# One block for three stages: last sums inverted later, an activation ahead of a root, another order text

## The chip, the cores and the metric

The kernel runs on one core of a Trainium2 chip. The metric is the device time of one execution, in microseconds (us), from start to end on that core. Five engines work side by side, each on its own queue of instructions: TensorE (PE), VectorE (DVE), ScalarE (ACT), GpSimd (POOL) and SyncE (SP, which only issues transfers). They meet only through semaphores. A block holds one list of instructions for each engine, and at its end all engines drain and wait for each other before the next block begins.

## The reference

Four sequences of 2048 rows of 256 numbers go through attention and then through two of eight experts. Cut to what matters:

```python
def _layernorm(x, axis=-1, eps=1e-05):
    m = jnp.mean(x, axis=axis, keepdims=True)
    v = jnp.var(x, axis=axis, keepdims=True)
    return (x - m) / jnp.sqrt(v + eps)

# attention: 16 heads of 16, causal
q = (x @ wq + bq).reshape(b, s, H, HD).transpose(0, 2, 1, 3)   # k, v alike
scores = jnp.where(causal, jnp.einsum('bhqd,bhkd->bhqk', q, k) * SCALE, -jnp.inf)
out = jnp.einsum('bhqk,bhkd->bhqd', jax.nn.softmax(scores, axis=-1), v)
return out.transpose(0, 2, 1, 3).reshape(b, s, d) @ wo + bo

# experts: the two best of 8 by the first row of each sequence
_, idx = jax.lax.top_k(x[:, 0, :] @ Wr + br, 2)
h = jax.nn.gelu(jnp.einsum('bsd,bkde->bkse', x, W1[idx]) + b1[idx][:, :, None, :], approximate=False)
o = jnp.einsum('bkse,bkef->bksf', h, W2[idx]) + b2[idx][:, :, None, :]
return jnp.sum(o, axis=1) / 2

x = x + _layernorm(attention(_layernorm(x)))
x = x + _layernorm(experts(_layernorm(x)))
```

## The kernel before, in words

The rows are cut into 16 chunks of 512 (four per sequence), numbered n = 0 to 15, with b = n // 4 and c = n % 4.

**Stage A** (`stage_a`) normalises each chunk, multiplies it by wq, wk and wv, and stores the products in DRAM. **Stage B** (`stage_b`) is the attention: eight pairs of groups of four heads each. PE multiplies queries and keys twice. The first product (line 622, into the tile b_ring of three banks) is only for the row maxima, which DVE takes with `tensor_reduce` (line 632, into b_pmax). The second (line 1392, into b_psS) gives the scores, ACT takes their exponentials (line 1349), and PE multiplies them with the values (line 1409, into b_psO). There are 640 steps of values.

In which order PE works these off is written out by hand in the text `ORDERS`, and every engine of stage B walks through the same text: 0 and 1 are a quarter of a score step in the upper or lower half of the array, a and b a maximum unit in that half, v a step of values, and p, q, r, y and l are pieces of the front. The **front** (class `Front`) is the beginning of stage C for the first sequence, run in the tail of stage B: p projects half a chunk, q and r take square roots, y turns half of a normalised chunk, l scores the experts.

The sums of the exponentials come out as a column of the values. For each pair, SP loads them (`load_sums`, line 231), DVE inverts them (`invert_sums`, line 236), SP stores the inverses (`store_inverses`, line 240). For the last pair this is done at the start of stage C.

**Stage C** (`stage_c`) has one step for each chunk n. PE: `hidden(n)` (line 1763, 16 multiplications into the two banks of c_psH, four pieces i), `outer(n)` (line 1776), `turn_y(n + 2)` (line 1742), `project(n + 4)` (line 1733). ACT: `gelu(n)` (line 1684, one activation per piece), the roots (line 99) of the chunks ahead, `copy_y(n + 2)` (line 1709), `root_ffn(n)` (line 99). DVE: `normalise_x1(n + 2)`, `add_attention(n + 3)`, `experts_end(n)` (lines 1616 to 1623 and the variance of the result), `take_projection(n + 4)`, `experts_out(n)`. PE's third piece of `hidden(n)` waits for the first gelu of the same chunk, because there are two banks. Gelu and square root lie in different tables of ACT, and between them a table is loaded (ACT_TABLE_LOAD).

Stages A and B share one block, and stage C has its own. ACT's last work in stage B is the copy of the last b_psO (line 1359) and a gelu of one column (line 1378) that brings the gelu table. ACT's first instruction in stage C is `act.sem_inc(gelu_done, 2)` (line 1711), for which the first piece of `hidden(0)` waits:

```python
            nc.scalar.activation(ready[:, :], consts.eps[:, :], ACT.Gelu)   # end of stage B
            ...
            act.sem_inc(gelu_done, 2)                                       # start of stage C
            for b, c in STEPS:
                n = b * NC + c
                if n < UNLED:
                    gelu(b, c, n)
                if ahead(b, c, 3):
                    roots(*ahead(b, c, 3))
                if ahead(b, c, 2):
                    copy_y(*ahead(b, c, 2))
                if n >= UNLED - 1 and n < LAST:
                    gelu(*ahead(b, c, 1))
                root_ffn(b, c, n)
```

With UNLED = 14, ACT's order at the end is gelu(12), roots(15), copy_y(14), root_ffn(12), gelu(13), copy_y(15), gelu(14), root_ffn(13), gelu(15), root_ffn(14), root_ffn(15).

Of the kernel before, what the change touches and what calls it, by code (L numbers as in the profile page):

```python
# [259 lines left out]
class Groups:  # L260
# [7 lines left out]
    def __init__(self, nc, ctx, qk_scr, v_scr):  # L268
        self.nc, self.qk_scr, self.v_scr = nc, qk_scr, v_scr
        self.ones_set = ctx.enter_context(nc.semaphore("g_ones_set"))  # L270
        self.ones_laid = ctx.enter_context(nc.semaphore("g_ones_laid"))
# [7 lines left out]
        self.nmax_set = ctx.enter_context(nc.semaphore("b_nmax_set"))  # L279
        self.vS = ctx.enter_context(nc.sbuf_tensor("g_v", [P, 2, NT, VROW], F32))  # L280
        self.loaded = [ctx.enter_context(nc.semaphore(f"g_loaded{p}")) for p in range(2)]
        self.early = [ctx.enter_context(nc.semaphore(f"g_early{h}")) for h in range(2)]
# [68 lines left out]
NPAIR = B * NG // 2  # L351
# [72 lines left out]
def leads_of(n):  # L424
# [9 lines left out]
    "0b011ab01a010a110aa010a1vba1010b0011v0101b0011b0101a1010bv01ab01vb0101a1010bbvb0101a101ab0v0b0b0101bav1a"  # L434
    "1a1010abva110b01b100bvab010101a10v1010a1100a10100b01a1va1010bva1010b010b1ava1010ba1010bv1a100b010b1ab010"
    "1abva1010b0101abvb0101ab0101ava1010ba1010bvba10101010bbbvab1010ab0110ba1010bv1a1b00101a0va11100010ba10b0"
    "1avvb01av1a1a100bb0v0101abb0101v01010101v0b1a10b0101ava1010b0101abv1a0b01010ba1vb0101a10b01avb0101a101a0"
    "bva1010b01a10bva1010b011ab0va10101a10b0bvb0101a1010bavba101a10100avab01010101av01010ba110a0101a1010bv10b"
    "a10v0b01a10101bva1b0010011av1ab0010101b1010vb0101ava10b011a100bva1010ba1010bva1010b0b011ab0101bavb00101a"
    "bva110b001a1vab0101001a1v10100b011a1a10b0v10b01ava1010a101a0bvb0101a1010bav1a101a100b0bvb0101aa1010bva10"  # L440
    "10b0101abva1010b0101abv1ab0101010bav1a0b100b0ba1a1v1a1010ba1v0b01ab010v10101ab001a10101010aav0101abv011a"
    "101abv0b0b0101abv1a1a010b010bavb0101a1010bav0b1a10b0101avb0101a1010bava1010b0101bava1010b0101abva1010b01"
    "01abvb01010b01a1avb0101a1010bava1010ba1010bv1a1001ab010bvb0010101a1av10101ab001b010101a10bv010b1bb0101bv",
    "10101ab010v0101ab0101b101010b0va1a1010bvb0101bb0101bv1a10b0101a0bva1010b011ab0va1010ba1vab010b0va110101a"
    "b0vb001a11010v1010ba10101010bavva1010b0b01a1va1010b01a10bvb0101a101ab0v1a100b01a10bva1010b01b0a1va1010b0"
    "101aavba1001ba1010bav0b011aa101ab0v01010ba101av1ab0101010v0101ab0101b01010101av1a0b10bb0101av1a100b0101a"
    "bva1010b01a10bv1a10b0101ab0vb0101a1010bav0b01a10101abvb01010b01ava101a10bv0b0b1010bav1a1a10b01ava1010ba1"
    "010bvb0101a1010bavb0101a10b01av0b0110b1a1b0vb001010ba11v10101a100aa1010101a0bva110b0v0b01a10101av0101ab0"
# [12 lines left out]
    "v0b1a010b1aa0ba1v1a100b1a10b0v1ab010b00v1a1b001a1v10101010aa10101a10b0v1a100bav1a10b00101abv1a0b01010ba1"
    "va1010b0101abv0b1a1010b01avb0101a1010bava1010b0101bava1010b0101abva1010b0101abvb01010b01a1avb0101ab0101a"
    "va1010b0101abvb0101a1010bava110101abv0b0010ba1v10101a100a01010b01a1vba1010v",
    "0ba101010b1va110b0001a1v10100ba1010101bavvb01010ba101avb0101a1010bavb0101a100ba1vb0101ab0101avb001a1101b"
    "0bvb00101a110av1010ab001110100b01a1vb0101abv1a0101a10b0bva1010b0101abva10101ab010bva1010b0101abvb0101a10"
    "10bbvab0101a1a10b0v0bb1a101a0b10ab0101v1010bab0va110b001a1v10101010bava11100010ba0101ava1010ba1vba1010b0"
    "10v1a0b01a1010bva1010b0101abv0b1a10b0101avb0101a1010bava1010b010b1av0b01a1a1010bvb0101a100ba1vb01a101010"
    "bavb0101ab0101ava1010b0101abvb0101a101a0bvb001a11a1va1b0010b0v0101ba1100b01010101bvb0011abv010ba10101vb0"
    "a1101010av0101a1010ba1010bvva1010b011ab0vb0101a0b01a1va1010b01a10bvb0101a1010bavb0011ba0101b1010bvba1010"
    "101a0v0101a1010ba1010bvvb0101ab0101av0b011a1a100bva1010ba1010bvb0101a1010bavb0101a10b01av0ba1010101abv1a"  # L470
    "010b1a010bbabv1a0b01a10b10b110b0bv0ba1101010bav0101ab0101v1a1100100ba1010bva1010bb010a1v0b011aa1010bva10"
    "10ba1010bv1a0b010b01a1va1010b0101abvb0101a1a100bv0b01a10101abva1010b0b011ava10101a10b0bva1010ba1010bvb01"
# [1366 lines left out]
```

## Time and profile before

| what | us |
|---|---|
| median of 3 runs | 1967.99 |
| lowest and highest | 1967.27 and 1971.41 |
| the profiled execution's own time | 1965.89 |
| its span, first to last instruction | 1964.20 |
| PE busy in the span | 1933.7 |
| DVE busy in the span | 1781.1 |
| ACT busy in the span | 1363.1 |

Stage A takes the first 210 us, stage B goes on to 1665.7 us, and stage C to the end. The profiled execution has 1.7 us around its span. Its ends of multiplications are modelled, so that PE can be shown busy while it goes slower than it could.

### The profile page before, as it was taken

What the parts mean: (1) busy time and instruction counts of PE and PEld (TensorE: products, weight loads), DVE (VectorE), ACT (ScalarE), POOL (GpSimd) and SP (SyncE); (2) the same over time, 40 slices, a digit from 0 to 9 for tenths busy, and PEclk for the clock granted to TensorE, in tenths of its full rate; (3) what the DMA queues carried; (4) which work ended last, traced back from release to release, by engine and by line L of the source; (5) the groups of instructions that cost most, each with busy time, mean ns of one, the idle gap of its engine ahead of it and who ended that gap; (6) DMA issues with size and microseconds to landing.
All of it is one profiled execution on the core that took longest, in us unless ns stands there. A gap on an engine that the chain in (4) does not pass through costs nothing. (4 is left out here: it accounts for less than half of the span.)

```text
span 1964.2 us, 39436 instructions
## 1 busy us (share of the span) xinstructions
PE 1933.7 (98%) x15684; PEld 848.7 (43%) x15684; DVE 1781.1 (91%) x3574; ACT 1363.1 (69%) x1655; POOL 295.1 (15%) x358
## 2 busy tenths in 40 slices
PE   9999999999999999999999999999999998999997
PEld 6655333333333333333333333333333342667665
DVE  7877899999999999999999999999999985799984
ACT  5766777777777777777777777777777768333432
POOL 4332201011111101010111111010101121322000
PEclk9999999999999999999999999999999999999999
DMA  6876716050415224050504152240505223344321
GB/s 179 252 230 201 151 39 105 7 95 9 94 27 82 52 48 90 14 94 8 94 9 94 26 82 56 45 86 17 93 7 109 80 75 120 85 127 126 94 72 43
DMA packets 151706, 162.93 MB, mean 83 GB/s; under 512 B 58466, under 2 KB 124386, under 8 KB 151522
## 3 DMA queue, kind: packets, MB, share of 16 engines
q1 hardware_dynamic: 146658, 151.98, 33.5%
q0 software_dynamic: 4864, 8.44, 1.8%
q8 instruction: 123, 2.02, 0.5%
q14 instruction: 61, 0.50, 0.1%
HBM read 100.03 MB, written 60.29 MB: 82 GB/s over the span
## 5 line engine op out<-in xcount | busy, mean ns | idle before, releaser
L632 DVE TENSOR_REDUCE b_pmax<-b_ring 128x1 f32<-128x512 f32 (+3 forms) x2264 | 1316.9, 645 | 45.6 <-PE b_ring L622 32.2
L1349 ACT ACTIVATE b_prob<-b_psS 128x1024 f32<-128x1024 f32 (+3 forms) x1280 | 1084.4, 895 | 334.4 <-PE b_psS L1392 330.6
L1392 PE MATMUL b_psS<-g_qT,g_kT 64*128 64x512 bf16 (+7 forms) x5120 | 809.3, 346 | 7.0 <-ACT b_prob L1349 5.5
L622 PE MATMUL b_ring<-g_kT,g_qT 64*128 64x512 bf16 (+3 forms) x2478 | 705.2, 347 | 0.1
L1409 PE MATMUL b_psO<-b_prob,g_v 128*32 128x512 f32 (+3 forms) x5120 | 596.4, 540 | 0.3 <-POOL b_prob L1319 0.3
L1392 PEld LDWEIGHTS b_psS<-g_qT,g_kT 64*128 64x128 bf16 (+1 forms) x5120 | 291.5, 94 | 315.9 <-ACT b_prob L1349 178.3
L622 PEld LDWEIGHTS b_ring<-g_kT,g_qT 64*128 64x128 bf16 x2478 | 221.4, 94 | 384.0 <-DVE b_pmax L632 317.4
L1319 POOL TENSOR_SCALAR_AFFINE_SELECT b_prob<-b_prob 128x512 f32<-128x512 f32 x256 | 163.0, 637 | 1281.6 <-ACT b_prob L1349 1281.4
L620 PE MATMUL b_ring<-later,query_of 64*128 64x128 bf16 x982 | 186.0, 219 | 0.8 <-ACT a_v L1104 0.5
L1409 PEld LDWEIGHTS b_psO<-b_prob,g_v 128*32 128x32 f32 x5120 | 102.9, 108 | 167.7 <-issue 131.3
L1763 PE MATMUL c_psH<-c_yT,c_w1e 128*128 128x512 f32 x256 | 116.2, 603 | 9.9 <-ACT c_hT L1684 7.3
L1173 PE MATMUL a_psQK<-c_cc,a_w 128*128 128x512 f32 x256 | 115.8, 599 | 1.2 <-ACT c_cc L1093 1.2
L1776 PE MATMUL c_psO<-c_w2e,c_hT 128*128 128x256 f32 x512 | 113.4, 380 | 0.0
L620 PEld LDWEIGHTS b_ring<-later,query_of 64*128 64x128 bf16 x982 | 85.5, 94 | 46.3 <-DVE b_pmax L632 20.8
L1776 PEld LDWEIGHTS c_psO<-c_w2e,c_hT 128*128 128x128 f32 x512 | 97.0, 190 | 18.7 <-issue 6.2
L1684 ACT ACTIVATE c_hT<-c_psH,c_b1e 128x512 f32<-128x512 f32 x64 | 43.2, 687 | 54.0 <-PE c_psH L1763 53.9
L1763 PEld LDWEIGHTS c_psH<-c_yT,c_w1e 128*128 128x128 f32 x256 | 48.3, 192 | 68.2 <-issue 52.2
L1173 PEld LDWEIGHTS a_psQK<-c_cc,a_w 128*128 128x128 f32 x256 | 47.1, 190 | 54.8 <-issue 53.8
L632 DVE TENSOR_REDUCE b_pmax<-a_ring 128x1 f32<-128x512 f32 (+4 forms) x72 | 42.3, 629 | 20.5 <-PE a_ring L622 20.5
L1187 PE MATMUL a_psV<-a_w,c_cc 128*128 128x256 f32 x256 | 60.4, 383 | 0.0
L99 ACT ACTIVATE c_ln_x_std<-c_ln_x_var,eps 128x4 f32<-128x4 f32 x12 | 3.6, 297 | 74.5 <-DVE c_ln_x_var L95 74.5
L982 DVE TENSOR_TENSOR a_parts<-c_inv,a_parts 128x2048 bf16<-128x2048 f32 x16 | 36.7, 2291 | 19.3 <-ACT a_parts L978 19.3
(162 smaller groups left out, 1058.6 us busy)
## 6 DMA issues: line engine op xcount, KB each, us to landing
qk_parts<-a_parts SPq DMA_DIRECT2D x64, 384.0 KB, 4.5
g_qT<-qk_parts SPq DMA_DIRECT2D x184, 128.0 KB, 4.7
g_kT<-qk_parts SPq DMA_DIRECT2D x184, 128.0 KB, 6.1
out_sums<-b_outT SPq DMA_DIRECT2D x64, 256.0 KB, 3.3
v_ones<-a_v SPq DMA_DIRECT2D x16, 544.0 KB, 5.7
g_v<-v_ones SPq DMA_DIRECT2D x32, 272.0 KB, 5.8
a_x<-in_L_attn_x SPq DMA_DIRECT2D x16, 512.0 KB, 5.2
c_x<-in_L_attn_x SPq DMA_DIRECT2D x15, 512.0 KB, 4.8
```

What stands on the lines that cost most here:

```text
L620: self.nc.tensor.matmul(to[:, w - P:w], consts.query_of[half:half + HALF, :], consts.later[half:half + HALF, :], start=True, stop=False, s ...
L622: ins_ = self.nc.tensor.matmul(to, groups.qT[own, g, h // 2, 0, t * P:(t + 1) * P], groups.kT[own, g, h // 2, 0, pc * CH:pc * CH + w], sta ...
L632: self.nc.vector.tensor_reduce(pmax[:, c % 2].rearrange("p (h t) n -> p h t n", t=TT)[:, heads[0]:heads[-1] + 1:2, qt, pc], bank[:, 0:k * ...
L1173: ins_ = nc.tensor.matmul(psQK[:, i % 2], w[:, t, k, m * P:(m + 1) * P], xT[:, n % 2, k], start=(k == 0), stop=(k == KD - 1))
L1187: ins_ = nc.tensor.matmul(psV[:, t], xT[:, n % 2, k, t * P:(t + 1) * P], w[:, 2, k], start=(k == 0), stop=(k == KD - 1))
L1319: nc.gpsimd.affine_select(out=tile, in_=tile, compare_op=ALU.is_ge, fill=0.0, base=0, pattern=[[0, HG], [1, P]], channel_multiplier=-1).th ...
L1349: nc.scalar.activation(prob[:, j % PBUF, 2 * s:2 * s + 2, off:CH], psS[:, 2 * s:2 * s + 2, off:CH], ACT.Exp).then_inc(exp_done, 1)
L1392: ins_ = nc.tensor.matmul(psS[:, 2 * s + p, off:CH], kT[own, g, s, ab, kt * P:(kt + 1) * P], qT[own, g, s, ab, c * CH + off:(c + 1) * CH], ...
L1409: ins_ = nc.tensor.matmul(psO[h * VW:(h + 1) * VW, off:CH], vS[:, g, kt, h * VC:h * VC + VW], prob[:, j % PBUF, h, off:CH], start=(kt == 0 ...
L1684: nc.scalar.activation(hT[:, e, m], psH[:, i % 2], ACT.Gelu, bias=experts[b % 2].b1[:, e, m:m + 1]).then_inc(gelu_done, 1)
L1763: ins_ = nc.tensor.matmul(psH[:, i % 2], experts[b % 2].w1[:, e, k, m * P:(m + 1) * P], yT[:, k, c], start=(k == 0), stop=(k == KD - 1))
L1776: ins_ = nc.tensor.matmul(psO[:, t], hT[:, e, m, t * P:(t + 1) * P], experts[b % 2].w2[:, e, m], start=(i == 0), stop=(i == 2 * KD - 1))
```

## The change

- `stage_c` gets the block of the other stages instead of one of its own, and all semaphores are now taken for the whole program. PE's first `hidden` waits for all turned pieces of the front and its choice of experts, and DVE's first `normalise_x1` for the turned pieces. The third chunk's input gets a semaphore of its own (`third_ld`), and SP's wait on the old one in `load_next_inputs` goes.
- `invert_sums` of the last pair moves from the start of DVE's stage C to the first step, between `add_attention(3)` and `experts_end(0)`.
- UNLED becomes 13: ACT's order at the end is gelu(12), roots(15), copy_y(14), **gelu(13)**, **root_ffn(12)**, copy_y(15), gelu(14), and the rest as before.
- `ORDERS` is another text with the same number of each sign.

```diff
-    def __init__(self, nc, ctx, qk_scr, v_scr):
+    def __init__(self, nc, ctx, sems, qk_scr, v_scr):
...
-    "b00v1010b0101ab0101ava0101a1010bav1a100b0101abv1a10b01010bav1a100b01a10bva1010b0101abvb01010b0b11bb01101"
-    "01a0vpp01010101vpp00110011vpp10101010v10101010vqp10101010v0101vv10101010v0101v01010101vrp01011010v101010"
-    "10vyy10100101vl01010101v10101010vyy10101010v01011010v01010101v1010101001010101v01010101v10101010vvv",
+    "b01010b111100vpp10101100vpp10100101vpp01010101v10101010vqp0101vv01010101v1010v01010101v01010101vrp010101"
+    "01v01011010vyy10101010vl01010101v01010101vyy01010101v10101010v0101010110100101v10101010v10101010vvv",
...
+        self.third_ld = sem("f_third_ld")
...
-            sp.dma_start(self.attn[:, :, :], self.chunks.x_t[2]).then_inc(self.chunks.x_ld[0], 16)
+            sp.dma_start(self.attn[:, :, :], self.chunks.x_t[2]).then_inc(self.third_ld, 16)
...
-        sp.wait_ge(self.chunks.x_ld[0], 2 * 16)
...
-        v.wait_ge(chunks.x_ld[c % 2], (c // 2 + 1) * 16)
+        if c == 2:
+            v.wait_ge(self.third_ld, 16)
+        else:
+            v.wait_ge(chunks.x_ld[c % 2], (c // 2 + 1) * 16)
...
-def stage_c(nc, consts, chunks, front, out):
+def stage_c(nc, block, sems, consts, chunks, front, out):
...
-        UNLED = LAST - 1
+        UNLED = LAST - 2
...
-        block = ctx.enter_context(nc.Block())
...
-                v.wait_ge(x_ld[c % 2], (b * 2 + c // 2 + 1) * 16)
+                v.wait_ge(x_ld[c % 2], (b * 2 + c // 2 + c % 2) * 16)
...
                 wait_for(v, y_turned, n - TURNED)
+                if n == TURNED:
+                    v.wait_ge(front.turned, 2 * TURNED)
...
-            chunks.invert_sums(v, NPAIR - 1)
             for b, c in STEPS:
...
                 n = b * NC + c
+                if n == 0:
+                    chunks.invert_sums(v, NPAIR - 1)
                 if n < LAST:
...
                     pe.wait_ge(w1_ld, (b + 1) * 16 * W_LOADS)
+                if n == 0:
+                    pe.wait_ge(front.turns_copied, 2 * TURNED)
+                    pe.wait_ge(idx_done, 1)
                 wait_for(pe, yT_done, n + 1 - TURNED)
...
+        block = outer.enter_context(nc.Block())
         with ExitStack() as ctx:
-            groups = Groups(nc, ctx, qk_scr, v_scr)
+            groups = Groups(nc, ctx, outer, qk_scr, v_scr)
             maxima = Maxima(nc, outer, consts, groups, nm_scr)
-            block = ctx.enter_context(nc.Block())
...
-        stage_c(nc, consts, chunks, front, out)
+        stage_c(nc, block, outer, consts, chunks, front, out)
```

## Rows read from the trace of the kernel before

**Rows 1.** Windows of stage B: PE, PEld, DVE, ACT, POOL busy; PEclk, DMA share, GB/s.

```profile
600.00:900.00 300.00, 299.41 (x2885) 110.09 (x2883) 289.04 (x519) 230.35 (x279) 33.11 (x52) 1.00 0.32 57
900.00:1200.00 300.00, 299.22 (x2870) 111.50 (x2866) 287.13 (x513) 232.36 (x279) 31.84 (x50) 1.00 0.28 51
1200.00:1500.00 300.00, 299.33 (x2904) 109.76 (x2903) 289.44 (x515) 231.16 (x284) 36.93 (x58) 1.00 0.32 61
```

**Rows 2.** Costliest groups, whole span: the maxima on DVE.

```profile
L632 DVE TENSOR_REDUCE b_pmax<-b_ring 128x1 f32<-128x512 f32 (+3 forms) x2264 | 1316.9, 645 | 45.6 <-PE b_ring L622 32.2
```

**Rows 3.** Timeline of PE after the join: start, us, line, idle before and releaser.

```profile
1668.25 8.73 PE L1763 MATMUL c_psH<-c_yT,c_w1e 128*128 128x512 f32 x16 [2.61 <-ACTq L1711]
...
1692.73 3.70 PE L1763 MATMUL c_psH<-c_yT,c_w1e 128*128 128x512 f32 x8 [1.07 <-ACT c_hT L1684]
...
1725.76 7.03 PE L1763 MATMUL c_psH<-c_yT,c_w1e 128*128 128x512 f32 x16
```

**Rows 4.** Timeline of ACT at the join.

```profile
1666.31 1.28 ACT L1378 ACT_TABLE_LOAD   x1
1667.61 0.20 ACT L1378 ACTIVATE b_ready<-eps 128x1 f32<-128x1 f32 x1
```

**Rows 5.** Lines 1807, 1711, 1568: queue instructions, ns min/median/max, first and last start.

```profile
L1807 ACTq DRAIN  x1: 2114/2114/2114, 1665.7 to 1665.7; - x1
L1711 ACTq EVENT_SEMAPHORE  x1: 17/17/17, 1668.1 to 1668.1; - x1
L1568 POOLq EVENT_SEMAPHORE  x4: 17/17/17, 1668.0 to 1668.4; - x4
```

**Rows 6.** Timeline of POOL at the join.

```profile
1668.19 9.26 POOL L1569 TENSOR_TENSOR c_cc<-c_cc,c_inv 128x1024 f32<-128x1024 f32 x4 [3.03 <-POOLq L1807]
```

**Rows 7.** Windows of 1 and 2 us, columns as in group 1.

```profile
1667.00:1668.00 1.00, 0.00 (x0) 0.00 (x0) 0.00 (x0) 0.80 (x2) 0.00 (x0) 1.00 0.68 262
...
1669.00:1670.00 1.00, 1.00 (x2) 0.33 (x1) 0.00 (x0) 0.00 (x0) 1.00 (x1) 0.50 0.04 11
...
1914.00:1916.00 2.00, 0.37 (x1) 0.30 (x2) 1.97 (x5) 1.99 (x3) 0.00 (x0) 1.00 0.00 0
```

**Rows 8.** Timeline of DVE in step 0 of stage C.

```profile
1670.94 0.95 DVE L236 RECIPROCAL b_pair_sums<-b_pair_sums 128x128 f32<-128x128 f32 x1 [22.62 <-DMA b_pair_sums<-out_sums]
1679.54 0.18 DVE L104 RECIPROCAL f_ln_x_rstd<-f_ln_x_std 128x4 f32<-128x4 f32 x1 [7.65 <-ACT f_ln_x_std L99]
...
1686.00 0.16 DVE L95 TENSOR_TENSOR f_ln_x_var<-f_ln_x_tmp 128x4 f32<-128x4 f32 x1
```

**Rows 9.** Timeline of PE in steps 13 and 14.

```profile
1909.19 3.60 PE L1763 MATMUL c_psH<-c_yT,c_w1e 128*128 128x512 f32 x8
1915.63 3.70 PE L1763 MATMUL c_psH<-c_yT,c_w1e 128*128 128x512 f32 x8 [2.84 <-ACT c_hT L1684]
...
1926.08 1.04 PE L1742 MATMUL c_psT<-ident,c_y 128*128 128x128 f32 x8
```

**Rows 10.** Timeline of ACT in steps 12 and 13.

```profile
1895.84 1.28 ACT L1684 ACT_TABLE_LOAD   x1 [1.78 <-PE c_psH L1763]
...
1902.32 1.28 ACT L99 ACT_TABLE_LOAD   x1
1903.62 0.30 ACT L99 ACTIVATE c_ln_a_std<-c_ln_a_var,eps 128x4 f32<-128x4 f32 x1
...
1909.39 1.02 ACT L1709 COPY c_yT<-c_psT 128x1024 f32<-128x1024 f32 x1
1913.28 0.30 ACT L99 ACTIVATE c_ln_f_std<-c_ln_f_var,eps 128x4 f32<-128x4 f32 x1 [2.87 <-DVE c_ln_f_var L95]
...
1919.37 0.69 ACT L1684 ACTIVATE c_hT<-c_psH,c_b1e 128x512 f32<-128x512 f32 x1 [1.03 <-PE c_psH L1763]
```

**Rows 11.** Timeline of DVE in step 13.

```profile
1913.61 0.18 DVE L104 RECIPROCAL c_ln_f_rstd<-c_ln_f_std 128x4 f32<-128x4 f32 x1 [0.36 <-ACT c_ln_f_std L99]
...
1916.59 1.38 DVE L110 TENSOR_SCALAR c_y<-c_x,c_ln_x_mean,c_ln_x_rstd 128x256 f32<-128x256 f32 x4
```

More of the change, by code:

```diff
@@ L266 @@
     LAID = 2 * 2 * HP
-    def __init__(self, nc, ctx, qk_scr, v_scr):
+    def __init__(self, nc, ctx, sems, qk_scr, v_scr):
         self.nc, self.qk_scr, self.v_scr = nc, qk_scr, v_scr
-        self.ones_set = ctx.enter_context(nc.semaphore("g_ones_set"))
-        self.ones_laid = ctx.enter_context(nc.semaphore("g_ones_laid"))
+        self.ones_set = sems.enter_context(nc.semaphore("g_ones_set"))
+        self.ones_laid = sems.enter_context(nc.semaphore("g_ones_laid"))
         self.ones = ctx.enter_context(nc.sbuf_tensor("g_ones", [P, S // P], BF16))
@@ L278, in __init__ @@
         self.nmT = ctx.enter_context(nc.sbuf_tensor("b_nmT", [P, 2, BLOCK], BF16))
-        self.nmax_set = ctx.enter_context(nc.semaphore("b_nmax_set"))
+        self.nmax_set = sems.enter_context(nc.semaphore("b_nmax_set"))
         self.vS = ctx.enter_context(nc.sbuf_tensor("g_v", [P, 2, NT, VROW], F32))
-        self.loaded = [ctx.enter_context(nc.semaphore(f"g_loaded{p}")) for p in range(2)]
-        self.early = [ctx.enter_context(nc.semaphore(f"g_early{h}")) for h in range(2)]
+        self.loaded = [sems.enter_context(nc.semaphore(f"g_loaded{p}")) for p in range(2)]
+        self.early = [sems.enter_context(nc.semaphore(f"g_early{h}")) for h in range(2)]
     def write_ones(self, pool):
@@ L439 @@
[L439 to L448, printed above, removed]
@@ new lines @@
+    "b0a1vb0010b0a11vb001001ba11vb00011101avb0101a1a10v0ba1010bva1010bb010a1vb0101a101ab0vb0101a10b01avb0101a"
+    "b0101ava1010b010ba1vba1010b1a010bav0b011aa1010bav1ab0010101abvb001a11010v1010b0011bb01010b01a1v1a100ba10"
+    "10bvb0101a101a0bv0b1ab010101avb0101a1010bav1a100b010ba1va1010b0101abvb0101a1a100bv0b01a1a1010bva1010b011"
+    "ab0va10101a10b0bvb0101a1010bavb0101a10b01avab0101a1vb0010b0a11vb001a11010bv1a1b000101a1010aav0101ab0101a"
+    "v",
+    "a110b00101va11110000aa0101a1010bva1010ba1010bv1a10b01010bavb010a10101abva1010ba1010bva110b00bvb00101a11a"
@@ new lines @@
+    "1010b0101ab0101avvb0101a10a1b0vb0101a1a100bva1010b0b011ava1010b01a10bvb0101a10b01avb0101a1010bv1aa0b101a"
+    "10b0v0bb1a101a10b0a1010abv0ba1101010bbv0101a1b001vb00011101ab01a10bv1a10b01av0b01010ba1va1010b0101abv0b0"
+    "11ab0101ava1010b0101abv0ba101010bv1a10b01avb0101a1010bav0b1a10b010ba1va1010b01a10bva1010b01b01avb0101a10"
+    "10bavb0101a1010bav0b01a1010aa1a1010ava110110b00av1010b0101a101a0bv1010bav",
+    "0b01010ba11v0101a1b001v0101a1010b1010bav10b01avb01010ba101ava1010b01a10bvb0101a1010bavb0101a1010bava1101"
@@ L513 @@
+    "110101a101010b01ava1010b1010bav0b01a1v1ab0100101abv1a100ba1010bvb0101a1010bavb0101ab0101avb0101a101ab0v0"
+    "b01010b111100vpp10101100vpp10100101vpp01010101v10101010vqp0101vv01010101v1010v01010101v01010101vrp010101"
+    "01v01011010vyy10101010vl01010101v01010101vyy01010101v10101010v0101010110100101v10101010v10101010vvv",
 )
@@ L1458, in sem @@
         def sem(name):
-            return ctx.enter_context(nc.semaphore(name))
+            return sems.enter_context(nc.semaphore(name))
         TURNED = 2
```

132 lines of the change are left out of this document (66 added, 66 removed).

## The prediction

> **What bounds the kernel now.** I read the windows first. In stage B, PE is shown busy for 299.2 to 299.4 us of every 300 and DVE for 287.1 to 289.4 [rows 1]. Which of the two sets the pace? PE's ends are modelled, so its 99.8% proves little. DVE's do not depend on a model, and the largest group of DVE, the maxima, has only 45.6 us of idle before its 2,264 instructions of 645 ns [rows 2]. So in stage B DVE is within about 4% of being the bound, and PE runs in step with it. The reader is to see there that neither engine alone can be relieved by the order text; only DVE's 45.6 us and what PE loses unseen are there to be won or lost.
>
> Then I read the timeline at the join of stages B and C, engine by engine. PE stands for 2.61 us before its first multiplication of stage C, and the releaser is not a computation but ACT's semaphore increment of line 1711 [rows 3]. ACT at that time loads the gelu table for 1.28 us and runs a one-column gelu that ends at 1667.61 + 0.20 = 1667.81 [rows 4]; its DRAIN, which is the end of the block, lasts from 1665.7 to 1667.8 [rows 5]. So the gap is ACT's table load, made visible by the drain. Behind the gap the 16 multiplications of `hidden(0)` take 8.73 us, where the same 16 take 7.03 us in step 3 [rows 3]. The windows say why: the granted clock reads 1.00 (2.4 GHz) at 1667 us, while PE does nothing, and 0.50 (1.2 GHz) at 1669 us [rows 7].
>
> Last I read the waits of PE in stage C. Nearly all of stage C is PE back to back. Two waits matter here: 1.07 us in step 1 [rows 3], and 2.84 us in step 13 [rows 9]. Both are for the first gelus of a chunk, which stand in ACT's queue behind a root that waits for DVE.
>
> **The change, part by part.**
>
> *The drain goes.* In one block, ACT issues line 1711 right behind the gelu of line 1378. Must it wait for that gelu to end? The DRAIN started at 1665.7, while the copy, the table load and the gelu had yet to run [rows 4, 5]. So the queue was already past them. POOL shows the same: its four increments of line 1568 went out from 1668.0 to 1668.4 [rows 5], while the first of its four operations, 9.26 us together, ran from 1668.19 [rows 6]. The increment then comes at about 1665.75. From 1711's increment (1668.06, within the 1668.1 of rows 5) to the multiplication at 1668.25 it is 0.19 us, so PE starts at about 1665.95 in place of 1668.25: −2.3 us. The bounds: at best PE starts as its values end, 1668.25 − 2.61 = 1665.64, −2.6; at worst the increment waits for 1667.81 and PE starts at 1668.0, −0.25. PE's other new waits cost nothing, because the front's work that they name lies some 13 us and more earlier. ACT is free at 1667.81, when the first piece of `hidden(0)` ends (a quarter of 7.03 us behind 1665.95 is 1667.7), so its gelu is 0.1 late, and PE needs it only a piece later.
>
> *The slow clock.* With PE's gap at 0.3 us, I expect the clock to stay at 2.4 GHz: 7.03 for 8.73, −1.7. The bound on the other side is 0. A gap alone does not decide it here: in step 13 PE stood 2.84 us and the window behind it still reads 1.00 [rows 7, 9]. So it is no certainty that a shorter gap keeps the clock, but nothing in the trace shows it fall while PE works.
>
> *The last sums.* Before, the reciprocal took 0.95 us at 1670.94, while DVE had been idle for 22.62 us and went on being idle until 1679.54 [rows 8]. Its cover is gone: it now stands behind `add_attention(3)`, whose last variance starts at 1686.00 [rows 8], and in front of `experts_end(0)`. DVE works there without a pause from 1679.54 to the variance of chunk 0, ACT's root waits for that, the gelu table and the first gelu of chunk 1 wait for the root, and PE waits 1.07 us for this gelu [rows 3]. So all of it falls on the path: +1.0 (bounds 0 and +1.2), and PE's wait in step 1 should read about 2.1. Behind it both engines are late by the same amount, so nothing absorbs it. Queued behind it are SP's store of the inverses (at about 1683 in the new times, some 11 us later than before) and POOL's loads of the third sequence's contexts. SP has only the first output store next in its queue, which comes later than that. The contexts are multiplied by PE only in step 4, over 60 us on. That is hidden.
>
> *Gelu(13) before root_ffn(12).* ACT has copied y(14) at 1909.39 + 1.02 = 1910.41 and then waits 2.87 us for DVE until 1913.28 [rows 10]. Afterwards the table load runs at 1910.41 to 1911.69 and the first gelu (0.69) ends at 1912.4. PE's first eight multiplications end at 1909.19 + 3.60 = 1912.79 [rows 9], so the wait of 2.84 is gone. What is late next? Two more table loads are the price, and they fall on the root of chunk 12. The last gelu of chunk 13 started at 1919.37; 2.84 earlier that is 1916.53. From such a gelu it takes 0.69, then from the table load at 1902.32 to the root at 1903.62 another 1.30, and 0.30 for the root [rows 10]: the root ends at 1918.8, and DVE's reciprocal, 1913.61 before [rows 11], starts at 1918.86, 5.25 later. The scaling of y(15), 1916.59 to 1917.97 before [rows 11], then ends at 1923.22. PE's `turn_y(15)` began at 1926.08 [rows 9], and wants it at 1923.24. That is just in time: cost 0 to 0.1. ACT's other new load, ahead of gelu(14), lies while PE works at the first two pieces of `hidden(14)`, 3.6 us; copy 1.02, load 1.28 and gelu 0.69 are 2.99, hidden too. Together −2.8. If the new load waited for PE's first piece, as it does in step 12 [rows 10], a wait of about 0.4 would remain: bounds −2.4 and −2.84.
>
> The page "ScalarE: Activation LUTs" of the Trainium skill, section "What ACT_TABLE_LOAD costs", speaks against this edit: every switch costs 1.28 us and a drain of 1.38 us. In this trace no drain is seen between the load at 1902.32 and the root at 1903.62 [rows 10]; with the page's price the root of chunk 12 would come 1.4 us later, `turn_y(15)` would wait for that, and the sum below would be smaller by 1.4.
>
> *The other text.* Both texts have 2,264 letters a and b, 5,120 digits and 640 v, so neither engine's own work changes. Next to each other on the same half of the array are 644 pairs before and 643 after, and the values stand in 621 and 627 runs. So PE has nothing from it. What can change is how evenly DVE is fed. I counted the maximum letters of each four steps of values up to step 616: their deviation is 2.71 before and 2.56 after, with a mean of 14.7; over eight steps it is 3.01 in both. If DVE's idle 45.6 us [rows 2] goes with the first count (6% less), that is −2.5; with the second, 0. I take the middle, −1.2. For the bounds I use how much equal stretches of the present text differ: DVE was busy 289.0, 287.1 and 289.4 us [rows 1], so a stretch of 300 us is off by 1.2, and stage B, some 1,450 us, by the square root of 4.8 times that, 2.6. Bounds: −4.2 and +3. The front in the tail has the same pieces in the same order, p later by one step of values, q where it was: within these bounds.
>
> The removed wait in `load_next_inputs` and the new `third_ld` name transfers issued far earlier: 0.
>
> **Sum:** −2.3 − 1.7 + 1.0 − 2.8 − 1.2 = −7.0. The profiled execution's span goes from 1964.2 to 1957.2 and its time from 1965.9 to 1958.9. It was 2.1 us below the median of the three runs, so the median goes from 1968.0 to 1961.0.
>
> **The rivals.**
>
> 1. *The increment waits for ACT.* If line 1711's increment waits for the one-column gelu, the gap stays at 2.35 us and the slow clock with it: −0.25 + 1.0 − 2.8 − 1.2 = −3.25, 1964.7. For it: the table load is really in that queue. Against it: the early DRAIN and POOL's increments [rows 5, 6].
> 2. *The clock still falls,* somewhere in `hidden(0)`, because PE's work at the end of stage B is thin: −5.3, 1962.7. For it: the clock did not fall with the longest wait of stage C, so something other than the gap takes part [rows 7, 9].
> 3. *A switch of table takes longer than its load,* because ACT has to drain for it. If it takes the 2.11 us of ACT's DRAIN [rows 5] and not 1.30, the root of chunk 12 is 0.8 later and `turn_y(15)` waits for it: −6.2, 1961.8. The row at 1903.62 is against it [rows 10]. The page named above has a rule of this kind.
> 4. *The text starves DVE.* The other side: if DVE's idle before the maxima grows from 45.6 us, the kernel gets slower from +5.8 us on (by more than the measurement can tell from +9.7 on). A quarter more idle, +11.4, gives −5.8 + 11.4 = +5.6, 1973.6. For it: DVE is within 4% of being the bound all through stage B, and every line of the text is new. Against it: the counts above are no worse.
> 5. *The edits work but the text eats them* in part: +2 to +5 in place of −1.2, 1964 to 1967.
>
> **How the numbers follow.** Forecast 0.60; rival 1: 0.07; rival 2: 0.11; rival 3: 0.04; rival 4: 0.04; rival 5: 0.14. What is likeliest is 1961.0. With the text's −4.2 it is 1958.0; past that I leave 1 in 10, so the low end is 1957. Rivals 1 to 3 and the lower half of rival 5 reach 1965.5. Some 0.2% (3.9 us) is what a measurement of this kernel can tell from no change. Faster by more than that, below 1964.1: the forecast and rivals 2 and 3 nearly whole, and a little of rival 1 and 5, 0.78. Within: most of rivals 1 and 5, 0.18. Slower: rival 4, 0.04.
>
> **What would show it.** In the profile after: PE's first line-1763 group starts 0.3 us behind its last values and takes 7.0 us, and no window near it reads below 1.00; the 0.95 us reciprocal stands between DVE's lines 95 and 1616, and PE's wait in step 1 reads 2.1; no wait of PE in step 13, two table loads more in ACT's list, `turn_y(15)` within 0.1 of `outer(13)`. For the text: DVE's idle before line 632 at 44 us or so, and last maximum some 1 us earlier. Wrong would be the sum if stage B's end moved by more than 3 us either way, or if PE's first group waited for line 1378.

## The result and the profile after

| | before | after |
|---|---|---|
| median of five runs of each, us | 1967.99 | 1957.04 |
| lowest and highest | 1967.21 and 1971.41 | 1956.24 and 1957.47 |
| profiled execution's own time | 1965.89 | 1957.42 |
| its span | 1964.2 | 1955.7 |

The ratio is 0.9941, with a 95% interval of 0.993 to 0.9951. The kernel became 10.9 us faster where 7.0 were forecast. The median of 1957.04 stands at the low end of the forecast range of 1957 to 1965.5, and the ratio times 1967.99 is 1956.4, just below it. The two profiled executions differ by less than the medians: their spans by 8.5 us, their times by 8.47.

The windows of stage B after stand against [rows 1], and the group of the maxima against [rows 2]. PE reads as full as before; DVE has 1.3 us less idle before its maxima.

```profile
600.00:900.00 300.00, 299.11 (x2891) 110.90 (x2890) 288.49 (x518) 233.25 (x283) 33.13 (x52) 1.00 0.29 54
900.00:1200.00 300.00, 299.48 (x2877) 109.36 (x2869) 290.14 (x519) 229.91 (x277) 31.98 (x51) 1.00 0.26 51
1200.00:1500.00 300.00, 299.23 (x2908) 110.93 (x2906) 288.37 (x514) 232.88 (x285) 36.83 (x58) 1.00 0.30 61
```

```profile
L633 DVE TENSOR_REDUCE b_pmax<-b_ring 128x1 f32<-128x512 f32 (+3 forms) x2264 | 1315.4, 646 | 44.3 <-PE b_ring L623 32.3
```

PE's timeline from the last values to step 14 answers to [rows 3, 9]. Start and duration come first, the idle time before the group and its releaser stand in the brackets.

```profile
1661.88 0.43 PE L1413 MATMUL b_psO<-b_prob,g_v 128*32 128x128 f32 x8 [0.28 <-POOL b_prob L1323]
1662.54 7.11 PE L1773 MATMUL c_psH<-c_yT,c_w1e 128*128 128x512 f32 x16 [0.23 <-ACTq L1718]
...
1686.36 3.70 PE L1773 MATMUL c_psH<-c_yT,c_w1e 128*128 128x512 f32 x8 [2.04 <-ACT c_hT L1691]
...
1818.05 3.70 PE L1773 MATMUL c_psH<-c_yT,c_w1e 128*128 128x512 f32 x8 [1.53 <-ACT c_hT L1691]
...
1892.39 3.70 PE L1773 MATMUL c_psH<-c_yT,c_w1e 128*128 128x512 f32 x8 [0.40 <-ACT c_hT L1691]
1903.71 7.03 PE L1773 MATMUL c_psH<-c_yT,c_w1e 128*128 128x512 f32 x16
1910.58 7.07 PE L1786 MATMUL c_psO<-c_w2e,c_hT 128*128 128x256 f32 x32
1917.52 1.09 PE L1749 MATMUL c_psT<-ident,c_y 128*128 128x128 f32 x8
1918.45 7.03 PE L1773 MATMUL c_psH<-c_yT,c_w1e 128*128 128x512 f32 x16
```

Three things are to be seen. The gap at the join is 0.23 us for 2.61, and `hidden(0)` behind it takes 7.11 us for 8.73. Step 1 waits 2.04 us for 1.07. And step 13 has no wait: its 16 multiplications, the group of 7.03 us at 1903.71, stand together. The windows at the join keep a granted clock of 1.00 (2.4 GHz), where [rows 7] fell to 0.50:

```profile
1662.00:1663.00 1.00, 0.77 (x9) 0.34 (x8) 0.00 (x0) 0.61 (x2) 1.00 (x1) 1.00 0.00 0
1663.00:1664.00 1.00, 1.00 (x4) 0.47 (x3) 0.00 (x0) 1.00 (x1) 1.00 (x1) 1.00 0.14 55
```

ACT's timeline shows that the table load did not go away. It now lies beside PE's first pieces, and the gelu of the first piece runs at 1664.60. At the end of stage C the order is the new one, against [rows 10]:

```profile
1662.38 0.59 ACT L1363 COPY b_outT<-b_psO 128x512 f32<-128x512 f32 x1 [1.35 <-PE b_psO L1413]
1662.98 1.28 ACT L1382 ACT_TABLE_LOAD   x1
1664.27 0.20 ACT L1382 ACTIVATE b_ready<-eps 128x1 f32<-128x1 f32 x1
1664.60 0.69 ACT L1691 ACTIVATE c_hT<-c_psH,c_b1e 128x512 f32<-128x512 f32 x1
...
1903.91 1.01 ACT L1716 COPY c_yT<-c_psT 128x1024 f32<-128x1024 f32 x1
1904.94 1.28 ACT L1691 ACT_TABLE_LOAD   x1
1906.23 0.69 ACT L1691 ACTIVATE c_hT<-c_psH,c_b1e 128x512 f32<-128x512 f32 x1
...
1911.48 1.28 ACT L99 ACT_TABLE_LOAD   x1
1912.78 0.30 ACT L99 ACTIVATE c_ln_f_std<-c_ln_f_var,eps 128x4 f32<-128x4 f32 x1
```

DVE's timeline has the moved reciprocal between the variance and the bias of `experts_end(0)`, as expected, against [rows 8, 11]. The last row scales y(15): it ends at 1917.47, and `turn_y(15)` begins at 1917.52.

```profile
1678.74 0.16 DVE L95 TENSOR_TENSOR f_ln_x_var<-f_ln_x_tmp 128x4 f32<-128x4 f32 x1
1678.82 0.94 DVE L236 RECIPROCAL b_pair_sums<-b_pair_sums 128x128 f32<-128x128 f32 x1
1679.68 0.23 DVE L1622 TENSOR_SCALAR c_b2half<-c_b2e 128x256 f32<-128x256 f32 x1
...
1916.09 1.38 DVE L110 TENSOR_SCALAR c_y<-c_x,c_ln_x_mean,c_ln_x_rstd 128x256 f32<-128x256 f32 x4
```

PE's rows cut the difference of the two spans into pieces. Each line is the same pair of events in both kernels:

| stretch | before | after | difference | forecast |
|---|---|---|---|---|
| start to the end of the last values | 1665.64 | 1662.31 | −3.33 | −1.2 |
| gap to `hidden(0)` | 2.61 | 0.23 | −2.38 | −2.3 |
| `hidden(0)` | 8.73 | 7.11 | −1.62 | −1.7 |
| its end to the second half of `hidden(1)` | 15.75 | 16.71 | +0.96 | +1.0 |
| from there to the second half of `hidden(12)` | 205.15 | 206.03 | +0.88 | 0 |
| from there to `hidden(13)` | 11.31 | 11.32 | +0.01 | 0 |
| `hidden(13)` to `hidden(14)` | 17.76 | 14.74 | −3.02 | −2.8 |
| from there to the end | 37.2 | 37.2 | 0.0 | 0 |

The sum is −8.5. So four of the five forecast terms hold within a quarter of a microsecond; the text is 2.1 us better, one item of +0.9 was not foreseen, and 2.5 us of the medians' difference are not in these two executions at all.

### The profile page after: what moved, and what is told of

It reads as the page before. It is cut to its first block, busy times and chain, and to the rows that moved or that the text cites. A ratio compares the mean times of both kernels' runs of the same rounds, so it can differ in the third digit from the quotient of the medians.

```text
span 1955.7 us, 39428 instructions
## 1 busy us (share of the span) xinstructions
PE 1928.3 (99%) x15684; PEld 846.7 (43%) x15684; DVE 1779.3 (91%) x3574; ACT 1365.4 (70%) x1657; POOL 295.7 (15%) x358
## 3 DMA queue, kind: packets, MB, share of 16 engines
q8 instruction: 123, 2.02, 0.4%
## 4 chain that ended last, share of the span: by engine, by line
PE 89%; DVE 6%; ACT 3%; issue 1%; POOL 0%; ACTq 0%; POOLq 0%; DVEq 0%
PE b_psO L1413 28%; PE b_psS L1396 24%; PE b_ring L623 17%; PE a_psQK L1177 6%; PE c_psH L1773 4%; PE a_psV L1191 3%; PE c_psO L1786 3%; ACT b_prob L1353 2%; PE b_ring L621 1%; DVE b_pmax L633 1%; PE c_psA L1740 1%; PE a_psT L1145 1%; PE b_ring L799 1%; DVE c_y L110 1%; DVE c_ln_f_stats L83 1%
## 5 line engine op out<-in xcount | busy, mean ns | idle before, releaser
L623 PE MATMUL b_ring<-g_kT,g_qT 64*128 64x512 bf16 (+3 forms) x2478 | 713.9, 347 | 0.4
```

The costliest lines, as they stand in the source:

```text
L623: ins_ = self.nc.tensor.matmul(to, groups.qT[own, g, h // 2, 0, t * P:(t + 1) * P], groups.kT[own, g, h // 2, 0, pc * CH:pc * CH + w], sta ...
```

## The experiments

The experiments ran in three groups, each beside executions of the kernel before, whose medians there were 1969.12 us (the first four experiments), 1969.30 (the next four) and 1968.84 (the last three). A difference of medians between kernels of different groups carries that spread, so the traces' rows stand beside it.

**The text alone.** The kernel before, with the new `ORDERS` and the semaphore of the third chunk's input.

```diff
-ORDERS = ( ... the old text ... )
+ORDERS = ( ... the new text ... )
+        self.third_ld = sem("f_third_ld")
```

> The kernel before with the new order text and the third input's own semaphore, and nothing else. Theory A (the part of the gain that the forecast missed is the text's): the last values of stage B start 3.3 us earlier than 1665.2, as in the profile after, and the whole is 3 to 4 us faster than before. Theory B (the text is worth the forecast 1.2 and the rest is a spread between executions of the kernel before): about 1 us faster. Theory C (what the profile does not show, some 2.5 us between the profiled difference of 8.5 and the difference of medians of 10.9, belongs to the text): 5 us or more faster.

Measured: median 1965.04 against 1969.12 for before beside it, ratio 0.9978 (0.9969 to 0.9988). From the first to the last values of stage B it is 1447.25 us, before 1451.41, after 1447.30. The waits at the join, in step 1 and in step 13 stand as in before. So the text is worth 4.2 us from the first values on, and 3.3 us of span, net of 0.8 us at its start (the new text has four more score digits ahead of the first v). The last values themselves start only 1.8 us earlier here (1663.43 for 1665.22), not the 3.3 expected: in this execution the granted clock was at 0.50 in stage A, from 11.7 to 15.1 us, and its first 16 multiplications of that stage took 8.80 us for 7.11. In the eight profiles with the new text and no such stretch the last values start 2.7 to 3.3 us earlier than before. The gain has no one place: compared at the starts of the values with the same number, the kernel after is 0.8 us late at the first, 1.6 early at number 240, 3.1 at 400 and 3.9 at 600, and it swings in between (0.5 early at 403).

**The gelu alone.** The kernel before, with one number changed.

```diff
-        UNLED = LAST - 1
+        UNLED = LAST - 2
```

> The kernel before with UNLED = 13 and nothing else. Theory A (a switch of table costs its load of 1.28 us and PE's wait in step 13 was all of the price): 2.8 to 3.0 us faster, no wait of PE in step 13, turn_y(15) at most 0.1 us behind outer(13). Rival (ACT drains for each switch, 1.4 us more): 1.4 to 1.6 us faster, with turn_y(15) late by 1.4 us.

Measured: 1963.87, ratio 0.9973 (0.9962 to 0.9984), and 14.74 us from `hidden(13)` to `hidden(14)`. The rows give 3.0 us back and the medians 5.3, with an interval of 3.2 to 7.5. That is the first sign that the wait of step 13 costs more in most executions than in the profiled one.

**The block alone.** The kernel after with the old text, UNLED = LAST − 1 and the last sums inverted ahead of the loop.

```diff
-        UNLED = LAST - 2
+        UNLED = LAST - 1
...
+            chunks.invert_sums(v, NPAIR - 1)
             for b, c in STEPS:
...
-                if n == 0:
-                    chunks.invert_sums(v, NPAIR - 1)
```

> The kernel after with the old text, UNLED = 14 and the last sums inverted first in DVE's stage C: of the change only the one block is left. Theory A (drain 2.3 us and slow clock 1.7 us both go): 4.0 us faster than before, PE's first multiplication of stage C some 0.3 us behind its last values, the first 16 at 7.0 us. Rival (the clock falls at the join whatever the gap): 2.3 us faster, the first 16 at 8.7 us.

Measured: 1964.45, ratio 0.9978 (0.9969 to 0.9987). `hidden(0)` starts 0.66 us behind the start of the last values and takes 6.95 us to `outer(0)`. The span is only 1.5 us shorter than before, where 4.0 were expected. The join gives back its 4.0, but steps 2 to 12 take 0.7 us more than in the profile of before, and step 13 takes 1.7 more. Step 13, in the same order as in before, shows in PE's timeline and in the windows what [rows 7, 9] do not:

```profile
1906.05 3.60 PE L1771 MATMUL c_psH<-c_yT,c_w1e 128*128 128x512 f32 x8
1912.48 5.40 PE L1771 MATMUL c_psH<-c_yT,c_w1e 128*128 128x512 f32 x8 [2.83 <-ACT c_hT L1689]
```

```profile
1913.00:1917.00 4.00, 4.00 (x7) 1.73 (x6) 1.78 (x6) 0.70 (x2) 0.00 (x0) 0.59 0.38 131
```

Behind the same wait (2.83 here, 2.84 before) the eight multiplications take 5.40 us in place of 3.70. The granted clock reads 0.59 as a mean of 1913 to 1917 us, most of which is at 1.2 GHz. So the clock can fall behind the wait of step 13. Three profiled executions have this wait: in before and in the text alone the clock stayed up, here it fell.

**The sums back ahead of the loop.** The kernel after with the third part undone, as in the diff above.

> The kernel after, with the last sums inverted first in DVE's stage C again, in the one block. Theory A (the reciprocal of 0.95 us has no cover between add_attention(3) and experts_end(0), and would have one in front of normalise_x1(2), where DVE is idle for 24.7 us): 1.0 us faster than after, PE's wait in step 1 at 1.1 us and not 2.0. Rival (the wait for the sums in DVE's queue comes late, and normalise_x1(2) with it): no faster than after.

Measured: 1956.81, ratio 0.9942 (0.9929 to 0.9956); the span is 1954.5 for 1955.7. Step 1 waits 1.14 us for 2.04. So moving the reciprocal costs the 0.9 to 1.0 us forecast, by the rows; in the medians it is lost among their 0.3%.

**The increment behind the one-column gelu.** This builds rival 1: the kernel after, with the increment made by the gelu that brings the table.

```diff
-            nc.scalar.activation(ready[:, :], consts.eps[:, :], ACT.Gelu)
+            nc.scalar.activation(ready[:, :], consts.eps[:, :], ACT.Gelu).then_inc(front.gelu_done, 2)
...
-            act.sem_inc(gelu_done, 2)
```

> The kernel after, but the increment of gelu_done that releases PE's first piece comes from the one-column gelu at the end of stage B and no longer from ACT's queue ahead of it: the first rival of the prediction, made on purpose, without a drain. It tells the gap from the clock. Theory A (the clock falls when PE stands for some 2 us behind the thin end of stage B): PE's gap grows from 0.2 to about 2.2 us, a low stretch stands behind it as in the kernel before, the first 16 multiplications take 8.6 us, and the whole is 3.7 us slower than after. Rival (the gap alone counts, the low clock needs the drain or a longer gap): 2.0 us slower than after, the first 16 at 7.0 us.

Measured: 1962.02, ratio 0.9966 (0.9954 to 0.9979), 5.0 us slower than the kernel after by the medians and 3.0 by the spans (1958.7 for 1955.7). The join costs 3.8 of it, the 3.7 expected; steps 2 to 12 are 0.9 us shorter here. PE's timeline and the windows:

```profile
1664.76 8.80 PE L1773 MATMUL c_psH<-c_yT,c_w1e 128*128 128x512 f32 x16 [2.31 <-ACT b_ready L1383]
```

```profile
1664.00:1665.00 1.00, 0.24 (x1) 0.27 (x2) 0.00 (x0) 0.60 (x2) 1.00 (x2) 0.99 0.64 248
1665.00:1668.00 3.00, 3.00 (x4) 1.04 (x4) 0.00 (x0) 0.00 (x0) 3.00 (x2) 0.50 0.07 22
```

With a gap of 2.31 us and no drain, no new block and no other change, `hidden(0)` takes 8.80 us and the clock falls to 0.50 (1.2 GHz). Gap and clock belong together: the term of −1.7 was the gap's second price. This also shows why the increment is early in the kernel after: an increment that stands alone in ACT's queue goes out at 1662.4, while the copy begins at 1662.38 and the table load is still to come.

**POOL's divisions left out.** The +0.9 between steps 1 and 12 was not foreseen. PE's waits for the first gelu of a chunk had grown in step 8 from 0.94 to 1.53 us and in step 4 from 0.94 to 1.06. The timelines of DVE and of POOL show what lies behind step 8. Before, POOL's division started as the scaling of y(9) was nearly over, and held a small instruction of the experts' choice:

```profile
1807.65 1.38 DVE L110 TENSOR_SCALAR c_y<-c_x,c_ln_x_mean,c_ln_x_rstd 128x256 f32<-128x256 f32 x4
1808.94 0.15 DVE L871 TENSOR_TENSOR c_rt<-c_psA,br 1x8 f32<-1x8 f32 x1
1809.12 0.15 DVE L876 TENSOR_REDUCE c_best<-c_rt 1x1 f32<-1x8 f32 x1
1809.31 1.94 DVE L879 SCALAR_TENSOR_TENSOR c_rt<-c_rt,c_best,place 1x8 f32<-1x8 f32 x1
```

```profile
1808.80 2.43 POOL L1569 TENSOR_TENSOR c_cc<-c_cc,c_inv 128x1024 f32<-128x1024 f32 x1 [5.07 <-DMA c_inv<-inverse_sums]
```

After, it falls into the scaling, which takes 3.47 us:

```profile
1801.68 3.47 DVE L110 TENSOR_SCALAR c_y<-c_x,c_ln_x_mean,c_ln_x_rstd 128x256 f32<-128x256 f32 x4
```

```profile
1802.65 2.35 POOL L1572 TENSOR_TENSOR c_cc<-c_cc,c_inv 128x1024 f32<-128x1024 f32 x1 [5.19 <-DMA c_inv<-inverse_sums]
```

The scaling ends at 1805.15, 0.15 us behind the division's end at 1805.00; the held instruction before ended at 1811.25, 0.02 behind. All eight divisions of this kind do so, in the trace of before and in that of after: one instruction of DVE lasts until 0.02 or 0.15 us behind the division's end. Not every instruction is held: lines 871 and 876 ran inside the division and took 0.15 us. The Trainium skill has a rule for it, on the page "SBUF — State Buffer", section "Who interferes with whom": DVE and GpSimd share a pair of ports that is locked for a whole instruction. By that rule, the trace agrees. The experiment leaves out most of this work, on top of the kernel with the sums early: for the chunks of the third and fourth sequence POOL divides only 8 of 512 columns, so the kernel no longer computes the whole result.

```diff
-                nc.gpsimd.tensor_tensor(cc[:, c], cc[:, c], inv[:, c], ALU.mult).then_inc(cc_done, 1)
+                own = slice(0, 8) if b > 1 else slice(0, CH)
+                nc.gpsimd.tensor_tensor(cc[:, c, :, own], cc[:, c, :, own], inv[:, c, :, own], ALU.mult).then_inc(cc_done, 1)
```

> The kernel with the last sums inverted early (the run sums_early), where POOL multiplies only 8 of 512 columns by the inverses for the chunks of the third and fourth sequence, so that most of that division is left out there. Theory A (each of these 2.35 us instructions of POOL holds up one instruction of DVE for 1.0 to 2.1 us, and DVE's lateness is what PE waits for in steps 3 to 9): no instruction of line 110 above 0.5 us in steps 1 to 8, PE's waits in these steps fall from 3.3 us together to under 0.5, the whole 3 us faster than sums_early. Rival (PE's waits there come from the table load and the choice of experts, whatever POOL does): under 1 us faster.

Measured: 1952.59, ratio 0.9915 (0.9899 to 0.9932), 4.2 us faster than the kernel with the sums early by the medians, 3.0 by the spans. From the second half of `hidden(1)` to the first of `hidden(12)` it is 198.25 us for 201.69, 3.4 less. PE's timeline:

```profile
1741.35 3.70 PE L1773 MATMUL c_psH<-c_yT,c_w1e 128*128 128x512 f32 x8 [0.40 <-ACT c_hT L1691]
1756.12 7.03 PE L1773 MATMUL c_psH<-c_yT,c_w1e 128*128 128x512 f32 x16
...
1814.80 3.70 PE L1773 MATMUL c_psH<-c_yT,c_w1e 128*128 128x512 f32 x8 [0.40 <-ACT c_hT L1691]
1829.57 7.03 PE L1773 MATMUL c_psH<-c_yT,c_w1e 128*128 128x512 f32 x16
```

Steps 5 and 9 no longer wait, and steps 4 and 8 wait the same 0.40 us, which is 0.3 more together than was expected to be left. So it is POOL that makes these waits unequal and long.

**POOL's divisions in four pieces.** All the work is done, but each piece of it is a quarter as large.

```diff
-                nc.gpsimd.tensor_tensor(cc[:, c], cc[:, c], inv[:, c], ALU.mult).then_inc(cc_done, 1)
+                for i in range(4):
+                    k, own = i // 2, slice(i % 2 * CH // 2, (i % 2 + 1) * CH // 2)
+                    ins_ = nc.gpsimd.tensor_tensor(cc[:, c, k, own], cc[:, c, k, own], inv[:, c, k, own], ALU.mult)
+                ins_.then_inc(cc_done, 1)
```

> The kernel sums_early with each of POOL's divisions in stage C cut into four instructions of a quarter, same result. Theory A (DVE gets its turn between two of POOL's instructions): DVE loses at most 0.6 us per step, the whole about 2 us faster than sums_early. Rival B (POOL takes the same time from DVE in four portions): no change within 0.5 us. Rival C (four starts on POOL cost more and DVE loses four times): 1 us slower or more.

Measured: 1955.17, ratio 0.9929 (0.9913 to 0.9946), span 1953.1. In step 8, DVE's and POOL's timelines:

```profile
1801.43 0.33 DVE L883 SCALAR_TENSOR_TENSOR c_rt<-c_rt,c_best,place 1x8 f32<-1x8 f32 x1
1801.79 0.15 DVE L886 TENSOR_REDUCE c_best<-c_rt 1x1 f32<-1x8 f32 x1
1801.97 0.47 DVE L890 TENSOR_SCALAR c_rt<-place,c_best 1x8 f32<-1x8 f32 x1
1802.47 0.64 DVE L892 TENSOR_TENSOR c_rt<-c_rt 1x8 f32<-1x8 f32 x1
...
1803.34 0.47 DVE L883 SCALAR_TENSOR_TENSOR c_rt<-c_rt,c_best,place 1x8 f32<-1x8 f32 x1
```

```profile
1801.02 2.77 POOL L1574 TENSOR_TENSOR c_cc<-c_cc,c_inv 128x256 f32<-128x256 f32 x4 [5.09 <-DMA c_inv<-inverse_sums]
```

The four pieces take POOL 2.77 us for 2.35, and no instruction of DVE is held by more than about 0.5 us. DVE does not lose only a quarter: four instructions are held here, by 0.1 to 0.5 us and 1.1 together, more than the 0.6 expected, but less than the 2.1 of the whole division above. From the second half of `hidden(1)` to the first of `hidden(12)` it is 199.73 us, for 201.69 with whole divisions: 2.0 us back (1.6 by the medians, 1.4 by the spans).

**ACT's wait for the experts' weights taken out** where PE's own wait covers it, to see whether it holds the gelus of steps 4, 8 and 12.

```diff
-                if c == 0:
-                    act.wait_ge(w1_ld, (b + 1) * 16 * W_LOADS)
```

> The kernel sums_early without ACT's wait for the first weights ahead of gelu in steps 0, 4, 8 and 12 (PE's pieces, for which these activations wait, come behind the same weights). Theory A (this wait keeps the gelu table from being loaded before PE's first piece in step 12): the load comes right behind the root instead of 1.8 us later, PE's wait of 0.4 us in step 12 goes, 0.4 us faster than sums_early. Rival (the load is tied to the activation's own wait): no change.

Measured: 1956.08, ratio 0.9931 (0.9914 to 0.9947), span 1955.0 for 1954.5 with the sums early. The table load comes right behind the root, as expected, and the wait in step 12 is gone, but steps 7 and 8 wait longer (by their starts 0.81 and 1.70 us), while POOL's divisions fall elsewhere (whether that is the reason was not tried). Inconclusive in the total.

**The kernel after once more**, beside the last two.

> The kernel after once more, unchanged, for a second profile and more executions beside the kernel before. If the clock explains what the profiles leave open (8.5 us between the profiled executions, 10.9 between the medians), all executions of it lie within 1.5 us of each other and show a mean clock of 0.998 or 0.999, while those of the kernel before show 0.996 to 0.998 and are the slower the lower it is. Ratio 0.994. If the spread has another cause, the time does not go with the clock.

Measured: 1957.35 (1956.65 to 1959.63), ratio 0.9944 (0.993 to 0.9957). Its profiled execution, at 1959.63 us, had the clock down in stage A, from 11.7 us on, as in the text alone, and its values start 1.8 us later for it. The other four lie within 1.7 us; so all five do not lie within the 1.5 us expected, and the mean clock of the slowest, 0.997, is below the range expected.

**All that helped together:** the kernel after with the sums early, the divisions in four pieces and without ACT's wait.

> The kernel after with the three edits that the runs so far point to: last sums inverted first in stage C's DVE list, POOL's divisions in four quarters, no wait for the weights on ACT. If they add: 1.0 + 2.0 + 0.5 = 3.5 us faster than after, 1953.5. If what POOL gives back is lost again in the later steps: 2 us faster.

Measured: 1953.98 (1953.55 to 1954.57), ratio 0.9926 (0.9912 to 0.9939), 3.4 us faster than the kernel after beside it, for the 3.5 expected. It beats both kernels.

**One more gelu ahead of its root:** the same with UNLED = LAST − 3.

> The kernel combined with UNLED = 12, so that gelu(12) too stands ahead of root_ffn(11). Theory A (the reordering pays only where PE waits for the root, and in step 12 nothing is left to win once the weight wait is gone): the root of chunk 11 comes 5.2 us later, DVE's out and y(14) with it, add_attention(15) is late, and PE waits for turn_y(14) or for the last gelus: 1 us slower or more than combined. Rival (DVE has the slack in steps 12 and 13, since no projection is left to take in): no change.

Measured: 1959.98, ratio 0.9956 (0.9942 to 0.9969), 6 us slower than without. PE's, DVE's and ACT's timelines:

```profile
1907.73 5.40 PE L1773 MATMUL c_psH<-c_yT,c_w1e 128*128 128x512 f32 x8 [3.73 <-ACT c_hT L1691]
```

```profile
1895.06 0.18 DVE L104 RECIPROCAL c_ln_f_rstd<-c_ln_f_std 128x4 f32<-128x4 f32 x1 [5.71 <-ACT c_ln_f_std L99]
```

```profile
1904.48 0.30 ACT L99 ACTIVATE c_ln_x_std<-c_ln_x_var,eps 128x4 f32<-128x4 f32 x1 [9.27 <-DVE c_ln_x_var L95]
```

Step 12 has no wait in either of the two kernels, and a long one comes in step 13: the root of chunk 11 is late, DVE stands 5.71 us for it, so `add_attention(15)` is late, and ACT stands 9.27 us for its variance ahead of the gelus of chunk 13. One step later there is no `add_attention` left behind the late root; that is why the edit is free in step 13 and costs 6 us in step 12. Here too the clock fell behind the wait (5.40 for 3.70).

## Why the forecast was right in direction and 4.0 us off

*The drain* (−2.3 forecast, −2.4 measured) and *the slow clock* (−1.7, −1.6): right, with the mechanism shown from the other side by the late increment. Rivals 1 and 2 fall.

*The last sums* (+1.0, measured +0.96 and 0.9 when undone): right. The wait in step 1 was forecast at 2.1 and reads 2.04.

*Gelu(13)* (−2.8, −3.0): right. The extra 0.2 is a matter of counting: the wait's label says 2.84, but from start to start the halves of `hidden(13)` were 6.44 us apart and are 3.43 when nothing waits, which is 3.01. Rival 3 falls: the table load at 1911.48 ends at 1912.76 and the root starts at 1912.78, with no drain between them. The page "ScalarE: Activation LUTs" of the Trainium skill, section "What ACT_TABLE_LOAD costs", which the prediction named, has a drain of 1.38 us for every switch; this trace shows 0.02 us. `turn_y(15)` was just in time, as forecast.

*The other text* (−1.2, measured −3.3) is one of the two steps that failed, and the prediction's own sign says so: it called its sum wrong if stage B's end moved by more than 3 us. The direction was right and the size was not. The term was half of what a count of letters suggested ("I take the middle"), and no run shows that this count measures time. DVE's idle before the maxima went down by 1.3 us, near the guess, but the distance from the first to the last maximum went down by 3.1 us (1391.5 for 1394.6), and by 2.9 to 3.2 us in each of the ten profiles with the new text. The rest is in no idle time: DVE's back-to-back instructions start before the former end, and these overlaps add up to 152.8 us for 149.8. That a late maximum loses its overlap as well as the idle time is argued, not shown: in the text alone, with the same distance, the overlaps are 151.2. Which passages of the text bring the gain was not found. The bounds of −4.2 and +3 held, but they do not follow from the numbers beside them: −1.2 with 2.6 either way gives −3.8 and +1.4.

*Nothing from step 2 to 12:* the prediction costed nothing there, and 0.9 us lies between the two profiles. POOL's divisions make the waits there, as the runs without them and with split ones show. But the 0.9 is not shown to come from the change. The stretch took 205.15 us in before and 205.7 to 205.9 in the three experiments whose kernels have the same order there (text, gelu and block alone). It took 206.03 in after and again 205.15 with the late increment, which keeps the order of after. The spread between executions is as large as the item.

*The other step that failed* is the last of the sum: "It was 2.1 us below the median of the three runs, so the median goes from 1968.0 to 1961.0." The distance was carried over to the kernel after, but it was the luck of one execution of before: its 1965.89 us lay below all three runs listed beside it (1967.27 and up). After, the profiled execution is 0.4 us above its median, and 2.1 + 0.4 = 2.5 us is what the medians moved more than the spans. The two failed steps, 2.1 and 2.5 us, make more than the whole miss of 4.0; the 0.9 took some of it away.

What was lucky? I had read in [rows 7, 9] that 2.84 us of standing did not lower the clock, and so priced that wait at 2.84 and no more. The 40 executions of before beside the experiments (one at 2153.57 us left out) and the ten of after read, by their mean granted clock:

| mean clock | before: executions, median us | after: executions, median us |
|---|---|---|
| 0.996 | 9, 1970.3 | 0 |
| 0.997 | 22, 1969.2 | 1, 1959.6 |
| 0.998 | 8, 1967.2 | 8, 1957.2 |
| 0.999 | 1, 1964.6 | 1, 1957.3 |

The profiled execution of before read 0.998; 31 of the 40 read less. By the rows, each time that the clock falls costs 1.7 us (8.73 for 7.11 at the join, 5.40 for 3.70 in step 13, 8.80 for 7.11 in stage A). That before loses its clock in step 13 too, in most executions, is argued. For it: the block alone, whose profile has that fall, has its profiled execution right at the median of eleven (1964.45), and the gelu alone gave 5.3 us in the medians for 3.0 in the rows. With that fall and the 0.7 us that steps 2 to 12 took more in the three experiments named above, I estimate 1965.89 + 1.7 + 0.7 = 1968.3 us for a usual execution of before; the 40 have a median of 1969.0. Against it: no profile of before shows the fall, and the text alone reads 0.997 without it, with a fall in stage A instead. Stage A's fall alone can hardly be the reason, because after has the same stage A and nine of its ten executions read 0.998 or more. The mean clock is also a rough sign: it counts a low stretch behind PE's last multiplication that costs nothing (5.9 us in the profile of before, 7.0 in that of after). Why the clock falls in some executions and not in others stays open.

## What to carry to other kernels

A wait of TensorE of 2 to 3 us can have two prices, its own length and the clock behind it, and the second is not in every execution. Before a forecast is made against a median, compare the profiled execution's time and mean clock with those of the others. Where it lies below all of them, its distance to the median is not to be carried over; ask first which wait could have cost more in the others.

An increment that depends on nothing should stand by itself in a queue and not behind a block's end, and work on GpSimd that runs beside VectorE is better issued in pieces. An activation may be put ahead of a root only where no chain that feeds the next step hangs on that root.

## What was not expected of the hardware

- A GpSimd division of 2.35 us holds one VectorE instruction until it ends (3.47 us for 1.38, 1.94 for 0.2), even one on 1 x 8 numbers; four pieces give back 2.0 us between steps 1 and 12.
- The granted clock fell at or behind waits of PE of 2.31, 2.61 (three profiles), 2.83 and 3.73 us, and in two of 13 profiles behind one of 1.19 us in stage A. It did not behind 2.84 us (two profiles) nor behind 2.02 to 2.05 us in step 1 (three).
- ACT's semaphore increment left its queue at 1662.4 us, ahead of a table load and a gelu that stood before it in the program and ended only at 1664.47 us.
